# Two of three Newton-Schulz transposes moved from TensorE to the DMA queue, the third product one step later, three buffers, and a reordered first tile

## The chip, the cores and the metric

The kernel runs on one core of one Trainium2 chip. The metric is the device time in microseconds (us); lower is better.

## The reference, cut to what matters

The whole block is an adaptive layer norm, a test-time-training attention (LaCT SwiGLU) and a mixture of experts, for 8 sequences of 256 tokens and 256 features. Three weight gradients per head and sequence, 48 matrices of 128x128, are orthogonalised by five Newton-Schulz steps:

```
for a, b, c in NS_COEFFS:              # 5 steps
    A = X @ jnp.swapaxes(X, 1, 2)      # first product, needs X transposed
    Bm = b * A + c * (A @ A)           # second product
    X = a * X + Bm @ X                 # third product
```

Before it stand `h1 = layernorm(x) * (1 + scale) + shift` and `qkv = silu(h1 @ w_qkv.T)`, behind it the updated weights `w + dw`, the outputs, and the experts.

## The kernel before

It is one program in which each engine's instruction list is written out by hand, in order, with semaphores between them. An engine works strictly through its list, so a wait holds back everything behind it.

**First stage.** The input is normalised on VectorE (`xn`), transposed on TensorE (`xn_turned`, L872), scaled on ScalarE (`h1_out`, L597) and rounded there to a high part `h1hi` (L602); GpSimd makes the low part `h1lo` (L412). The product with `w_qkv` (L949) is three products for each tile of 128 tokens: high times high, low times high, high times low weights. Tile 0 begins after the transposes of sequences 0 and 1 and after `spin(4)` (L864), four matmuls whose result nobody reads. ScalarE makes the bfloat16 identities `identb` and `aI` (L653, L655) after `h1_out(1)`.

**Newton-Schulz.** The 48 matrices are 12 groups of 4 (`NGRP = 12`, `MPG = 4`), so 5 steps make `NR = 60` units n; group g = n % 12. The loop over r is a pipeline. In step r TensorE issues: the first product of unit r from `XT` (L1057, 4 matmuls), the second of unit r-1 from `Ar` (L1068, 4), the third of unit r-2 (L1081 and L1082, 8), and the transpose of the new X of unit r-3 (L1097, 4), which the first product of unit n+12 needs. ScalarE evicts the first product to `Ar` (L751) and the third to `X` (L759); VectorE makes `Br` (L1455) and evicts the transpose from PSUM to `XT` (L1464). `Ar` and `Br` have two buffers each. From unit 48 on nothing is transposed for a next step; there GpSimd adds X to the gradient (L547), and TensorE transposes the sum (L1040).

**SyncE's list.** It issues the DMAs in this order: the inputs; `weights(0)` and `weights(1)` (raw expert weights, 384 KB each); after GpSimd's `ga_ok` a small store and two broadcasts of 1,024 KB each into `wog` (L366); then `weights(2)`, `weights(3)`, `weights(4)`; then the DMAs of the expert stage. `raw` has two buffers, so `weights(j)` waits for GpSimd's `w_prep` number j-1, which GpSimd reaches in `split_weights(j-2)` (L523, L525), after the load j-2 has landed:

```
def weights(j):
    if j >= 2:
        sp.wait_ge(S["w_prep"], j - 1)
    sp.dma_start(raw[:, j % 2, :], moew_d[:, j, :]).then_inc(...)
```

Of the kernel before, what the change touches and what calls it, by code (L numbers as in the profile page):

```python
# [20 lines left out]
F32 = mybir.dt.float32  # L21
# [53 lines left out]
def build(nc, x_d, c_d, wmod_d, qkvw_d, w02_d, w1_d, wnat_d, wo_d, onw_d, gate_d, ident_d, moew_d, comb_d, out_d):  # L75
    ctx = ExitStack()
    with ctx:
# [53 lines left out]
        def carve(start, names):  # L131
# [27 lines left out]
        (XT, Ar, Br), end = carve(R_tmp, [  # L159
            ("XT", [P, NMAT, P], BF16), ("Ar", [P, 2, BLK], BF16), ("Br", [P, 2, BLK], BF16)])  # L160
        assert end <= R_wo
# [11 lines left out]
        assert end <= R_tmp + 20480  # L173
        wsq = [at("wsq0", [P, 6, P], F32, R_tmp + 16384), at("wsq1", [P, 6, P], F32, R_q + 12288)]
        (raw,), end = carve(R_tmp + 20480, [("raw", [P, 2, WCOLS], F32)])
# [56 lines left out]
        def bank(i):  # L232
# [5 lines left out]

            "const", "ident_ok", "silu_c", "mod_ps", "mod_sb", "mod_ok", "mod2_sb", "mod2_ok", "ga_ps", "ga_sb", "ga_ok", "wo_ok", "st_ga", "ld_ga", "wog_ok", "wn_ss", "wn_ok",

# [4 lines left out]

            "up_ps", "sig", "b_sg", "b_u", "b_ds", "b_dhb", "b_hid", "b_t", "b_dg", "b_kl", "b_vl", "dw_ps", "dw_sb",
            "xb_ok", "f_ss", "g_sq", "f_s7",

            "f_ps", "f_sum", "f_norm", "f_b", "f_inv", "x_init", "x_init_p", "t0_ps", "t0_a", "t0_v", "t_ps", "t_sb", "a_ps", "a_sb", "b_ps", "b_sb", "x_ps", "x_sb",
            "w_ok", "wt_ps", "wt_sb", "wsq_ok", "rss_ok", "rsq_ok", "ws_pow", "ws_chain", "ws_pool", "w_scale", "w_scale_p",  # L250
# [46 lines left out]
        def root_of(b):  # L297
            return b // 2 + 1 if b < 6 else b - 2

        def first_xt_ps(g):  # L300
# [36 lines left out]
        def _(sp):  # L337
# [30 lines left out]
            for j in range(2, CPG):  # L368
                weights(j)
            for n in range(NU):  # L370
                wg, blk, c, tok = unit(n)
                for half in range(2):
                    if n == half * (NBLK // 2) * CPG:
                        sp.wait_ge(S["ld_ga"], 16 * NH)
                        sp.wait_ge(S["combT_ok"], 2 * (half + 1))
                        cols = slice(half * T // 2, (half + 1) * T // 2)
                        sp.dma_start(comb_d[:, cols], combT[:, cols]).then_inc(S["st_comb"], 16)
                        sp.wait_ge(S["st_comb"], 16 * (half + 1))
                if n in turn:
# [18 lines left out]
        def _(po):  # L398
# [143 lines left out]
            for g in range(NGRP):  # L542
                if g == NGRP - 5:
                    row_roots(0)
                po.wait_ge(S["x_sb"], NGRP * (NS_STEPS - 1) + g + 1)
                wv = dw[:, g * MPG:(g + 1) * MPG, :]
                po.tensor_tensor(wv, wv, X[:, g * MPG:(g + 1) * MPG, :], ALU.add).then_inc(S["w_ok"], 1)  # L547
# [36 lines left out]
        def _(ac):  # L584
# [60 lines left out]
            ac.wait_ge(S["mod_ok"], 2)  # L645
            h1_out(0)
            for t in range(NT):
                blk, i = divmod(t, 4)
                if t % TPB == 0 and t // TPB + 1 < B:
                    h1_out(t // TPB + 1)  # L650
                if t == 0:
                    ac.wait_ge(S["ld_id"], 16)
                    ac.activation(identb[:, :], ident[:, :], ACT.Copy).then_inc(S["ident_ok"], 1)  # L653
                    for k in range(NS_STEPS):
                        ac.activation(aI[:, k, :], ident[:, :], ACT.Copy, scale=NS[k][0]).then_inc(S["ident_ok"], 1)  # L655
                if t < NT:
# [86 lines left out]
            for r in range(NGRP * NS_STEPS + 2):  # L743
# [3 lines left out]
                if n < NGRP * NS_STEPS:  # L747
                    ac.wait_ge(S["a_ps"], n + 1)
                    if n >= 2:
                        ac.wait_ge(S["b_sb"], n - 1)  # L750
                    ac.activation(Ar[:, n % 2, :], bank(n % 2), ACT.Copy, scale=NS[n // NGRP][1]).then_inc(S["a_sb"], 1)  # L751
                for g in TURN_AT.get(r - 1, ()):
                    if g % 2 == 0:
                        first_turned(g)
                n = r - 2
                if n >= 0:
                    g = n % NGRP
                    ac.wait_ge(S["x_ps"], n + 1)
                    ac.activation(X[:, g * MPG:(g + 1) * MPG, :], bank(4 + n % 2).rearrange("p (a d) -> p a d", d=P),  # L759
                                  ACT.Copy).then_inc(S["x_sb"], 1)  # L760
                if r == NGRP * NS_STEPS - 5:
# [87 lines left out]
        def _(pe_):  # L849
# [80 lines left out]
            for t in range(NT + 1):  # L930
                blk, i = divmod(t, 4)
                if t % TPB == 0 and t // TPB + 1 < B:
                    xn_turned(t // TPB + 1)
                if t == 0:
                    spin(4)
                if t < NT:
# [4 lines left out]
                    pe_.wait_ge(S["h1_hi"], b + 1)  # L941
                    for k, (h_, w_) in enumerate(((h1hi, qkvhi), (h1lo, qkvhi), (h1hi, qkvlo))):
                        if k == 1:
                            pe_.wait_ge(S["h1_lo"], b + 1)
                        for c in range(KC):
                            if t == 0 and k != 1:
                                pe_.wait_ge(S["qw_hi" if k == 0 else "qw_lo"], c + 1)
# [84 lines left out]
            def weights_turned(g):  # L1032

                pe_.wait_ge(S["w_ok"], g + 1)
                if g >= 2:
                    pe_.wait_ge(S["wt_sb"], g - 1)
                else:
                    pe_.wait_ge(S["t_sb"], NR - NGRP)
                for a in range(MPG):
# [3 lines left out]
            for r in range(NR + 2):  # L1043
                n = r
                if n < NR:
                    g = n % NGRP
                    if n >= NGRP:
                        pe_.wait_ge(S["t_sb"], n + 1 - NGRP)
                    else:
# [10 lines left out]
                if 0 <= n < NR:  # L1060
# [5 lines left out]
                    for a in range(MPG):  # L1066
                        Am = Ar[:, n % 2, a * P:(a + 1) * P]
                        last = mm(bank(2 + n % 2)[:, a * P:(a + 1) * P], Am, Am, start=True, stop=True)  # L1068
                    last.then_inc(S["b_ps"], 1)
                n = r - 2  # L1070
                if 0 <= n < NR:
                    g = n % NGRP
                    pe_.wait_ge(S["b_sb"], n + 1)
                    if n >= 2:
                        pe_.wait_ge(S["x_sb"], n - 1)
                    else:
                        pe_.wait_ge(S["t0_v" if n else "t0_a"], 3)
                    for a in range(MPG):
                        o = bank(4 + n % 2)[:, a * P:(a + 1) * P]
                        Xm = X[:, g * MPG + a, :]  # L1080
                        mm(o, aI[:, n // NGRP, :], Xm, start=True, stop=False)  # L1081
                        last = mm(o, Br[:, n % 2, a * P:(a + 1) * P], Xm, start=False, stop=True)  # L1082
                    last.then_inc(S["x_ps"], 1)
                n = r - 3
                if 0 <= n < NR - NGRP:
                    g, m = n % NGRP, NGRP + n
                    pe_.wait_ge(S["x_sb"], n + 1)
                    if n >= 2:
                        pe_.wait_ge(S["t_sb"], n - 1)
                    if n in (0, 6):  # L1090
# [56 lines left out]
            for g in range(NGRP - 4, NGRP - 2):  # L1147
                weights_turned(g)
            pe_.wait_ge(S["x_sb"], NR)
            outputs(0)  # L1150
# [96 lines left out]
        def _(ve):  # L1247
# [89 lines left out]
            def gate_products(b):  # L1337

                i = b % 2
                ve.tensor_tensor(hid[i][:, :, :], sg[:, :, :], hid_ps(i), ALU.mult).then_inc(S["b_hid"], 1)  # L1340
                ve.tensor_tensor(dhb[i][:, :, :], sg[:, :, :], dh_ps(i), ALU.mult).then_inc(S["b_dhb"], 1)

# [100 lines left out]
            for r in range(NR + 1):  # L1443
# [6 lines left out]
                if 0 <= n < NR:  # L1450
                    ve.wait_ge(S["b_ps"], n + 1)
                    if n >= 2:
                        ve.wait_ge(S["x_ps"], n - 1)
                    _, b_, c_ = NS[n // NGRP]
                    ve.scalar_tensor_tensor(out=Br[:, n % 2, :], in0=bank(2 + n % 2), scalar=c_ / (b_ * b_), in1=Ar[:, n % 2, :],  # L1455
                                            op0=ALU.mult, op1=ALU.add).then_inc(S["b_sb"], 1)
                if r == 1:
                    ve.wait_ge(S["g_sq"], 1)
                    ve.tensor_reduce(fss[:, 6 * (B - 1):], gsq[:, :, :], AX.X, ALU.add).then_inc(S["f_s7"], 1)
                n = r - 3  # L1460
                if 0 <= n < NR - NGRP:
                    g, m = n % NGRP, NGRP + n
                    ve.wait_ge(S["t_ps"], n + 1)
                    ve.tensor_copy(XT[:, g * MPG:(g + 1) * MPG, :], xt_ps(m)).then_inc(S["t_sb"], 1)  # L1464
# [228 lines left out]
```

## Time and profile before

| | |
|---|---|
| median of 3 runs | 683.43 us (682.58 to 685.45) |
| the profiled execution's own time | 680.91 us |
| its span, first to last instruction | 679.1 us |
| TensorE busy | 652.2 us (96%) |
| VectorE, ScalarE, GpSimd busy | 475.2, 337.0, 227.4 us |
| mean granted clock of TensorE | 0.994 |

The span is what the trace covers; 1.8 us of the execution's own time lie around it. The busy share is an average over very unlike stages: Newton-Schulz takes roughly 120 to 199 us of the span, the experts everything from 295 us on.

### The profile page before, as it was taken

Reading aid. Unit: us, or ns where it says so; the run is one execution under the profiler, and the core shown is the slowest. Engines: PE = TensorE matmul, PEld = TensorE weight load, DVE = VectorE, ACT = ScalarE, POOL = GpSimd, SP = SyncE. Lnnn points to the kernel's source line nnn. Section 1 sums busy time; section 2 is a strip of 40 time slices with the busy share of each in tenths; the row PEclk is TensorE's granted clock in tenths of the full one; section 3 lists DMA queues with packets and bytes.
Section 4 is the critical chain, followed back from the end, with each engine's and each line's share of the span. In section 5 each row is a group of like instructions: output and inputs, shape, how many; then the busy total and the mean of one; then the engine's idle time right before and its main releaser. Section 6 shows DMA issues by size and latency. Waiting matters only on the chain.

```text
span 679.1 us, 11544 instructions
## 1 busy us (share of the span) xinstructions
PE 652.2 (96%) x4146; PEld 561.1 (83%) x4146; DVE 475.2 (70%) x925; ACT 337.0 (50%) x721; POOL 227.4 (33%) x221
## 2 busy tenths in 40 slices
PE   8999998799978999999999999999999999999997
PEld 7889898699966888888888888888888888888885
DVE  6988878899987787774457665566656565555545
ACT  3778699799976864532332222332222332222331
POOL 4578868858267641241003310123002330000000
PEclk7999999999999999999999999999999999999999
DMA  8000000150000000340023322243122342212132
GB/s 327 5 1 1 1 2 3 45 173 27 2 2 0 2 1 1 102 116 29 19 80 92 114 84 70 75 125 109 63 64 84 109 115 71 62 64 69 55 91 111
DMA packets 23095, 43.58 MB, mean 64 GB/s; under 512 B 3544, under 2 KB 5856, under 8 KB 22912
## 3 DMA queue, kind: packets, MB, share of 16 engines
q1 hardware_dynamic: 22624, 42.26, 19.8%
q8 instruction: 34, 0.56, 0.3%
q10 hardware_dynamic: 416, 0.59, 0.3%
q14 instruction: 21, 0.17, 0.1%
HBM read 40.60 MB, written 2.24 MB: 63 GB/s over the span
## 4 chain that ended last, share of the span: by engine, by line
PE 76%; DVE 10%; ACT 5%; POOL 5%; issue 2%; DMA 2%; DVEq 0%; SPq 0%; ACTq 0%; POOLq 0%
PE ps L1143 38%; PE ps L1220 19%; PE ps L949 3%; PE ps L1057 2%; PE ps L1068 2%; PE ps L1081 2%; PE ps L1082 2%; PE ps L990 2%; PE ps L1097 2%; PE ps L1186 1%; DVE x L1583 1%; ACT junk L712 1%; PE ps L1166 1%; POOL qk L433 1%; PE ps L918 1%
## 5 line engine op out<-in xcount | busy, mean ns | idle before, releaser
L842 ACT ACTIVATE sgm<-ps,zero 128x512 f32<-128x512 f32 x100 | 68.9, 690 | 273.0 <-PE ps L1143 273.0
L1143 PE MATMUL ps<-h2hi,whi 128*128 128x512 f32 x400 | 156.1, 390 | 0.0
L1143 PE MATMUL ps<-h2lo,whi 128*128 128x512 f32 x400 | 155.6, 389 | 0.0
L1143 PE MATMUL ps<-h2hi,wlo 128*128 128x512 f32 x400 | 155.6, 389 | 0.0
L1634 DVE TENSOR_TENSOR am<-sgm,ps 128x512 f32<-128x512 f32 x88 | 60.5, 688 | 135.6 <-ACT sgm L842 135.6
L523 POOL CAST whi<-raw 128x768 fp32r<-128x768 f32 x25 | 21.7, 866 | 242.0 <-DMA raw<-in_moew 242.0
L1143 PEld LDWEIGHTS ps<-h2lo,whi 128*128 128x128 f32 x400 | 75.1, 188 | 15.7
L1143 PEld LDWEIGHTS ps<-h2hi,whi 128*128 128x128 f32 x400 | 75.1, 188 | 15.5
L1143 PEld LDWEIGHTS ps<-h2hi,wlo 128*128 128x128 f32 x400 | 75.1, 188 | 15.3
L1643 DVE TENSOR_TENSOR pm<-am,cw 128x512 f32<-128x512 f32 x88 | 74.9, 851 | 5.2 <-DMA cw<-combine 2.8
L1220 PE MATMUL ps<-ahi,whi 128*128 128x512 f32 x200 | 77.9, 390 | 0.1
L1220 PE MATMUL ps<-alo,whi 128*128 128x512 f32 x200 | 77.8, 389 | 0.0
L1220 PE MATMUL ps<-ahi,wlo 128*128 128x512 f32 x200 | 77.8, 389 | 0.0
L1598 DVE TENSOR_TENSOR alo<-pm,ahi 128x512 fp32r<-128x512 f32 x100 | 74.7, 747 | 0.2
L832 ACT ACTIVATE ahi<-pm 128x512 fp32r<-128x512 f32 x100 | 62.3, 623 | 1.8 <-DVE pm L1643 1.0
L525 POOL TENSOR_TENSOR wlo<-raw,whi 128x768 fp32r<-128x768 f32 x25 | 47.6, 1905 | 2.0
L1220 PEld LDWEIGHTS ps<-ahi,whi 128*128 128x128 f32 x200 | 37.5, 188 | 8.3 <-DVE alo L1598 0.5
L1455 DVE SCALAR_TENSOR_TENSOR Br<-ps,Ar 128x512 bf16<-128x512 f32 x60 | 41.4, 690 | 4.2 <-PE ps L1068 3.1
L1220 PEld LDWEIGHTS ps<-alo,whi 128*128 128x128 f32 x200 | 37.5, 188 | 7.8
L1220 PEld LDWEIGHTS ps<-ahi,wlo 128*128 128x128 f32 x200 | 37.5, 188 | 7.7
L751 ACT ACTIVATE Ar<-ps 128x512 bf16<-128x512 f32 x60 | 35.5, 593 | 4.1 <-DVE Br L1455 2.5
L759 ACT ACTIVATE X<-ps 128x512 bf16<-128x512 f32 x60 | 35.9, 598 | 2.8 <-PE ps L1082 0.8
(212 smaller groups left out, 1187.0 us busy)
## 6 DMA issues: line engine op xcount, KB each, us to landing
raw<-in_moew SPq DMA_DIRECT2D x25, 384.0 KB, 3.9
cw<-combine SPq DMA_DIRECT2D x32, 256.0 KB, 3.2
cw<-combine SPq DMA_DIRECT2D x16, 224.0 KB, 2.9
cw<-combine SPq DMA_DIRECT2D x16, 192.0 KB, 2.8
cw<-combine SPq DMA_DIRECT2D x16, 160.0 KB, 2.7
wog<-combine SPq DMA_DIRECT2D x2, 1024.0 KB, 7.0
cw<-combine SPq DMA_DIRECT2D x16, 128.0 KB, 3.0
out<-x1T SPq DMA_DIRECT2D x8, 256.0 KB, 3.7
```

The costliest lines, as they stand in the source:

```text
L523: po.tensor_copy(whi[wg % 2][:, c, :], raw[:, j % 2, :]).then_inc(S["w_hi"], 1)
L525: po.tensor_tensor(wlo[wg % 2][:, c, :], raw[:, j % 2, :], whi[wg % 2][:, c, :].bitcast(F32), ALU.subtract).then_inc(S["w_prep"], 1)
L751: ac.activation(Ar[:, n % 2, :], bank(n % 2), ACT.Copy, scale=NS[n // NGRP][1]).then_inc(S["a_sb"], 1)
L759: ac.activation(X[:, g * MPG:(g + 1) * MPG, :], bank(4 + n % 2).rearrange("p (a d) -> p a d", d=P), ACT.Copy).then_inc(S["x_sb"], 1)
L832: ac.activation(ahi[:, n % 4, :], pm[:, n % 3, :], ACT.Copy).then_inc(S["e_hi"], 1)
L842: ac.activation(sgm[:, n % 2, :], gate_bank(n), ACT.Silu, bias=zero[:, :]).then_inc(S["e_sg"], 1)
L1143: last = mm(o, w_, a_[:, kc, tok], start=(kc == 0 and k == 0), stop=(kc == KC - 1 and k == 2))
L1220: last = mm(bank(6 + f), w_, a_, start=(c == 0 and k == 0), stop=(c == CPG - 1 and k == 2))
L1455: ve.scalar_tensor_tensor(out=Br[:, n % 2, :], in0=bank(2 + n % 2), scalar=c_ / (b_ * b_), in1=Ar[:, n % 2, :], op0=ALU.mult, op1=ALU.add) ...
L1598: ve.tensor_tensor(alo[:, n % 3, :], pm[:, n % 3, :], ahi[:, n % 4, :].bitcast(F32), ALU.subtract).then_inc(S["e_lo"], 1)
L1634: ve.tensor_tensor(am[:, n % 2, :], sgm[:, n % 2, :], lin_bank(n), ALU.mult).then_inc(S["e_a"], 1)
L1643: ve.tensor_tensor(pm[:, n % 3, :], am[:, n % 2, :], cw[:, k % 3, :], ALU.mult).then_inc(S["e_p"], 1)
```

## The change

- **Transposes.** `BY_DMA` is the list of units n from 13 to 47 that 3 does not divide: 24 units. Their X is transposed into `XT` by `dma_start_transpose`, issued by SyncE, one for each unit (128x512 bfloat16, 128 KB). The other 24 (`ON_PE`) stay on TensorE and VectorE. SyncE's new loop stands behind `weights(4)`. Four semaphores (`xt_ld0` to `xt_ld3`) let four such DMAs be in flight.
- **Third product.** For units 14 to 47 it is issued in step n+3 and no longer in n+2, with the transpose, where there is one, in step n+4.
- **Buffers.** `Ar` and `Br` have three (`DEEP = 3`); `wsq0` moves to other SBUF bytes, since `Ar` and `Br` now lie where it was.
- **Evictions.** X of units 16, 20, ... 44 (8 units, `ON_VECTOR`) is evicted by VectorE and no longer by ScalarE.
- **First tile.** `spin(4)` is removed; sequence 1 is transposed after tile 0's high product and no longer ahead of it; ScalarE makes the identities ahead of `h1_out(1)`. For all tiles the product with the low input comes last. Two semaphore increments that nobody waits for are removed.

```diff
-            ("XT", [P, NMAT, P], BF16), ("Ar", [P, 2, BLK], BF16), ("Br", [P, 2, BLK], BF16)])
+            ("XT", [P, NMAT, P], BF16), ("Ar", [P, 3, BLK], BF16), ("Br", [P, 3, BLK], BF16)])
...
+        DEEP = 3
+        def lag(n):
+            return 3 if 14 <= n < NGRP * (NS_STEPS - 1) else 2
+        def evicted_at(r):
+            return [n for n in (r - 3, r - 2) if 0 <= n < NGRP * NS_STEPS and n + lag(n) == r]
+        def turned_at(r):
+            return [n for n in (r - 4, r - 3) if 0 <= n < NGRP * (NS_STEPS - 1) and n + lag(n) + 1 == r]
+        BY_DMA = [n for n in range(13, NGRP * (NS_STEPS - 1)) if n % 3]
+        ON_PE = [n for n in range(NGRP * (NS_STEPS - 1)) if n not in BY_DMA]
+        ON_VECTOR = range(16, NGRP * (NS_STEPS - 1), 4)
...
             for j in range(2, CPG):
                 weights(j)
+            for k, n in enumerate(BY_DMA):
+                g = n % NGRP
+                if k >= 4:
+                    sp.wait_ge(*turned_by(BY_DMA[k - 4]))
+                sp.wait_ge(*made(n))
+                sp.dma_start_transpose(XT[:, g * MPG:(g + 1) * MPG, :], X[:, g * MPG:(g + 1) * MPG, :]).then_inc(turned_by(n)[0], 16)
...
             h1_out(0)
+            ac.wait_ge(S["ld_id"], 16)
+            ac.activation(identb[:, :], ident[:, :], ACT.Copy).then_inc(S["ident_ok"], 1)
+            for k in range(NS_STEPS):
+                ac.activation(aI[:, k, :], ident[:, :], ACT.Copy, scale=NS[k][0]).then_inc(S["ident_ok"], 1)
...
-                    if n >= 2:
-                        ac.wait_ge(S["b_sb"], n - 1)
-                    ac.activation(Ar[:, n % 2, :], bank(n % 2), ACT.Copy, scale=NS[n // NGRP][1]).then_inc(S["a_sb"], 1)
+                    if n >= DEEP:
+                        ac.wait_ge(S["b_sb"], n + 1 - DEEP)
+                    ac.activation(Ar[:, n % DEEP, :], bank(n % 2), ACT.Copy, scale=NS[n // NGRP][1]).then_inc(S["a_sb"], 1)
...
-                if t == 0:
-                    spin(4)
...
-                    for k, (h_, w_) in enumerate(((h1hi, qkvhi), (h1lo, qkvhi), (h1hi, qkvlo))):
-                        if k == 1:
+                    for k, (h_, w_) in enumerate(((h1hi, qkvhi), (h1hi, qkvlo), (h1lo, qkvhi))):
+                        if k == 2:
                             pe_.wait_ge(S["h1_lo"], b + 1)
+                        if t == 0 and k == 1:
+                            xn_turned(1)
...
                     if n >= NGRP:
-                        pe_.wait_ge(S["t_sb"], n + 1 - NGRP)
+                        pe_.wait_ge(*turned_by(n - NGRP))
...
+                for n in [n for n in evicted_at(r) if n in ON_VECTOR]:
+                    g = n % NGRP
+                    ve.wait_ge(S["x_ps"], n + 1)
+                    ve.tensor_copy(X[:, g * MPG:(g + 1) * MPG, :], bank(4 + n % 2).rearrange("p (a d) -> p a d", d=P)).then_inc(S["x_sv"], 1)
```

`made(n)` is the semaphore and count that say that X of unit n is written; `turned_by(n)` is the same for its transpose.

## Rows read from the trace of the kernel before

**Rows 1.** Windows: length, busy of PE, PEld, DVE, ACT, POOL, clock, DMA, GB/s.

```profile
152.40:182.10 29.70, 29.70 (x536) 29.70 (x534) 29.14 (x54) 28.86 (x54) 15.22 (x13) 1.00 0.06 16
...
256.00:679.00 423.00, 417.53 (x1870) 345.18 (x1868) 258.98 (x463) 132.73 (x217) 58.75 (x43) 1.00 0.26 79
```

**Rows 2.** Groups by line from 152.4 to 181.3 us, Newton-Schulz steps 25 to 50.

```profile
L1455 DVE SCALAR_TENSOR_TENSOR Br<-ps,Ar 128x512 bf16<-128x512 f32 x27 | 18.7, 692 | 0.6
L759 ACT ACTIVATE X<-ps 128x512 bf16<-128x512 f32 x26 | 15.5, 597 | 0.8
L751 ACT ACTIVATE Ar<-ps 128x512 bf16<-128x512 f32 x26 | 15.4, 591 | 0.0
...
L1464 DVE COPY XT<-ps 128x512 bf16<-128x512 bf16 x26 | 11.1, 426 | 0.0
L1097 PE MATMUL ps<-identb,X 128*128 128x128 bf16 x105 | 10.3, 219 | 0.0
```

**Rows 3.** Timeline of TensorE: first products of units 16, 25, 51 and 58.

```profile
142.14 0.39 PE L1057 MATMUL ps<-XT 128*128 128x128 bf16 x4
...
152.45 0.39 PE L1057 MATMUL ps<-XT 128*128 128x128 bf16 x4
...
181.48 0.39 PE L1057 MATMUL ps<-XT 128*128 128x128 bf16 x4
...
190.69 0.39 PE L1057 MATMUL ps<-XT 128*128 128x128 bf16 x4
```

**Rows 4.** Timeline of SyncE's queue: the broadcasts, weights(2) to weights(4), and weights(4) alone.

```profile
139.37 1.02 SPq L366 DMA_DIRECT2D wog<-combine  x2
140.71 12.20 SPq L357 DMA_DIRECT2D raw<-in_moew  x3
...
152.59 0.33 SPq L357 DMA_DIRECT2D raw<-in_moew  x1
```

**Rows 5.** Timeline of GpSimd: split_weights(2), and the next start on load 4.

```profile
149.83 0.82 POOL L523 CAST whi<-raw 128x768 fp32r<-128x768 f32 x1 [6.48 <-DMA raw<-in_moew]
150.74 1.82 POOL L525 TENSOR_TENSOR wlo<-raw,whi 128x768 fp32r<-128x768 f32 x1
...
155.74 0.82 POOL L523 CAST whi<-raw 128x768 fp32r<-128x768 f32 x1 [0.52 <-DMA raw<-in_moew]
```

**Rows 6.** DMA issues: size of each, median us from issue to landing.

```profile
raw<-in_moew SPq DMA_DIRECT2D x25, 384.0 KB, 3.9
...
cw<-combine SPq DMA_DIRECT2D x16, 128.0 KB, 3.0
...
combine<-combT SPq DMA_DIRECT2D x2, 64.0 KB, 1.9
```

**Rows 7.** Timeline of the first tile, ScalarE and TensorE.

```profile
11.29 0.63 ACT L602 ACTIVATE h1hi<-h1T 128x512 fp32r<-128x512 f32 x1
...
10.96 1.12 PE L872 MATMUL ps<-ident,xn 128*128 128x128 f32 x4 [0.82 <-DVE xn L1271]
11.87 1.92 PE L864 MATMUL ps<-ones 128*128 128x128 f32 x8
13.44 1.64 PE L949 MATMUL ps<-qkvhi,h1hi 128*128 128x512 f32 x4
...
16.63 0.87 PE L949 MATMUL ps<-qkvhi,h1hi 128*128 128x512 f32 x4
```

**Rows 8.** Windows of the clock, columns as in rows 1.

```profile
9.00:12.00 3.00, 2.12 (x9) 1.76 (x10) 2.83 (x4) 1.65 (x3) 1.76 (x3) 0.50 1.01 420
...
15.00:16.00 1.00, 1.00 (x6) 0.86 (x5) 1.00 (x7) 0.00 (x0) 1.00 (x2) 0.71 1.01 403
...
200.00:202.00 2.00, 0.42 (x2) 0.43 (x3) 2.00 (x5) 1.95 (x3) 1.33 (x1) 1.00 0.00 0
```

**Rows 9.** Timeline of tile 8's second and third product on TensorE.

```profile
37.65 0.99 PE L949 MATMUL ps<-qkvhi,h1lo 128*128 128x512 f32 x4 [1.46 <-POOL h1lo L412]
38.47 0.87 PE L949 MATMUL ps<-qkvlo,h1hi 128*128 128x512 f32 x4
```

More of the change, by code:

```diff
@@ L173, in build @@
         assert end <= R_tmp + 20480
-        wsq = [at("wsq0", [P, 6, P], F32, R_tmp + 16384), at("wsq1", [P, 6, P], F32, R_q + 12288)]
+        wsq = [at("wsq0", [P, 6, P], F32, R_x1T + T * 4 - 6 * P * 4), at("wsq1", [P, 6, P], F32, R_q + 12288)]
         (raw,), end = carve(R_tmp + 20480, [("raw", [P, 2, WCOLS], F32)])
@@ L237, in build @@
             "ld_x0", "ld_xa", "ld_xb", "ld_xc", "ld_mod", "ld_mod2", "ld_id", "ld_qkv0", "ld_qkv1", "ld_c", "ld_wn", "ld_w", "ld_raw0", "ld_raw1", "st_out",
-            "const", "ident_ok", "silu_c", "mod_ps", "mod_sb", "mod_ok", "mod2_sb", "mod2_ok", "ga_ps", "ga_sb", "ga_ok", "wo_ok", "st_ga", "ld_ga", "wog_ok", "wn_ss", "wn_ok",
+            "const", "ident_ok", "silu_c", "mod_ps", "mod_ok", "mod2_sb", "mod2_ok", "ga_ps", "ga_sb", "ga_ok", "wo_ok", "st_ga", "ld_ga", "wog_ok", "wn_ss", "wn_ok",
             "stat1", "agg1", "var1", "rs_ok", "xn_ok", "tr_ps", "h1_ok", "h1_hi", "h1_lo", "qw_hi", "qw_lo",
@@ L244, in build @@
             "lr_z", "lr_e", "lr_c", "lr_ok",
-            "up_ps", "sig", "b_sg", "b_u", "b_ds", "b_dhb", "b_hid", "b_t", "b_dg", "b_kl", "b_vl", "dw_ps", "dw_sb",
+            "up_ps", "sig", "b_sg", "b_u", "b_ds", "b_t", "b_dg", "b_kl", "b_vl", "dw_ps", "dw_sb",
             "xb_ok", "f_ss", "g_sq", "f_s7",
-            "f_ps", "f_sum", "f_norm", "f_b", "f_inv", "x_init", "x_init_p", "t0_ps", "t0_a", "t0_v", "t_ps", "t_sb", "a_ps", "a_sb", "b_ps", "b_sb", "x_ps", "x_sb",
+            "f_ps", "f_sum", "f_norm", "f_b", "f_inv", "x_init", "x_init_p", "t0_ps", "t0_a", "t0_v", "t_ps", "t_sb", "xt_ld0", "xt_ld1", "xt_ld2", "xt_ld3", "a_ps", "a_sb", "b_ps", "b_sb", "x_ps", "x_sb", "x_sv",
             "w_ok", "wt_ps", "wt_sb", "wsq_ok", "rss_ok", "rsq_ok", "ws_pow", "ws_chain", "ws_pool", "w_scale", "w_scale_p",
@@ L298, in root_of, with turned_by, made @@
             return b // 2 + 1 if b < 6 else b - 2
+        DEEP = 3
[8 more added lines that the diff above has]
+        ON_VECTOR = range(16, NGRP * (NS_STEPS - 1), 4)
+        def turned_by(n):
+            if n not in BY_DMA:
+                return S["t_sb"], ON_PE.index(n) + 1
+            k = BY_DMA.index(n)
+            return S[f"xt_ld{k % 4}"], 16 * (k // 4 + 1)
+        def made(n):
+            vector = len([k for k in ON_VECTOR if k <= n])
+            return (S["x_sv"], vector) if n in ON_VECTOR else (S["x_sb"], n + 1 - vector)
         def first_xt_ps(g):
@@ L544, in _ @@
                     row_roots(0)
-                po.wait_ge(S["x_sb"], NGRP * (NS_STEPS - 1) + g + 1)
+                po.wait_ge(*made(NGRP * (NS_STEPS - 1) + g))
                 wv = dw[:, g * MPG:(g + 1) * MPG, :]
@@ L650, in _ @@
                     h1_out(t // TPB + 1)
-                if t == 0:
[L652 to L655, printed above, removed]
                 if t < NT:
@@ L754, in _ @@
                         first_turned(g)
-                n = r - 2
-                if n >= 0:
+                for n in evicted_at(r):
                     g = n % NGRP
-                    ac.wait_ge(S["x_ps"], n + 1)
-                    ac.activation(X[:, g * MPG:(g + 1) * MPG, :], bank(4 + n % 2).rearrange("p (a d) -> p a d", d=P),
-                                  ACT.Copy).then_inc(S["x_sb"], 1)
+                    if n not in ON_VECTOR:
+                        ac.wait_ge(S["x_ps"], n + 1)
+                        ac.activation(X[:, g * MPG:(g + 1) * MPG, :], bank(4 + n % 2).rearrange("p (a d) -> p a d", d=P),
+                                      ACT.Copy).then_inc(S["x_sb"], 1)
                 if r == NGRP * NS_STEPS - 5:
@@ L931, in _ @@
                 blk, i = divmod(t, 4)
-                if t % TPB == 0 and t // TPB + 1 < B:
+                if t and t % TPB == 0 and t // TPB + 1 < B:
                     xn_turned(t // TPB + 1)
-                if t == 0:
-                    spin(4)
                 if t < NT:
@@ L941, in _ @@
                     pe_.wait_ge(S["h1_hi"], b + 1)
-                    for k, (h_, w_) in enumerate(((h1hi, qkvhi), (h1lo, qkvhi), (h1hi, qkvlo))):
-                        if k == 1:
+                    for k, (h_, w_) in enumerate(((h1hi, qkvhi), (h1hi, qkvlo), (h1lo, qkvhi))):
+                        if k == 2:
                             pe_.wait_ge(S["h1_lo"], b + 1)
+                        if t == 0 and k == 1:
+                            xn_turned(1)
                         for c in range(KC):
-                            if t == 0 and k != 1:
+                            if t == 0 and k < 2:
                                 pe_.wait_ge(S["qw_hi" if k == 0 else "qw_lo"], c + 1)
@@ L1037, in weights_turned @@
                 else:
-                    pe_.wait_ge(S["t_sb"], NR - NGRP)
+                    pe_.wait_ge(S["t_sb"], len(ON_PE))
                 for a in range(MPG):
@@ L1066, in _ @@
                     for a in range(MPG):
-                        Am = Ar[:, n % 2, a * P:(a + 1) * P]
+                        Am = Ar[:, n % DEEP, a * P:(a + 1) * P]
                         last = mm(bank(2 + n % 2)[:, a * P:(a + 1) * P], Am, Am, start=True, stop=True)
                     last.then_inc(S["b_ps"], 1)
-                n = r - 2
-                if 0 <= n < NR:
+                for n in evicted_at(r):
                     g = n % NGRP
@@ L1074, in _ @@
                     if n >= 2:
-                        pe_.wait_ge(S["x_sb"], n - 1)
+                        pe_.wait_ge(*made(n - 2))
                     else:
@@ L1081, in _ @@
                         mm(o, aI[:, n // NGRP, :], Xm, start=True, stop=False)
-                        last = mm(o, Br[:, n % 2, a * P:(a + 1) * P], Xm, start=False, stop=True)
+                        last = mm(o, Br[:, n % DEEP, a * P:(a + 1) * P], Xm, start=False, stop=True)
                     last.then_inc(S["x_ps"], 1)
[L1084 to L1089, printed above, removed]
+                for n in [n for n in turned_at(r) if n in ON_PE]:
+                    g, m = n % NGRP, ON_PE.index(n)
+                    pe_.wait_ge(*made(n))
+                    if m >= 2:
+                        pe_.wait_ge(S["t_sb"], m - 1)
                     if n in (0, 6):
@@ L1148, in _ @@
                 weights_turned(g)
-            pe_.wait_ge(S["x_sb"], NR)
+            pe_.wait_ge(*made(NR - 1))
             outputs(0)
@@ L1339, in gate_products @@
                 i = b % 2
-                ve.tensor_tensor(hid[i][:, :, :], sg[:, :, :], hid_ps(i), ALU.mult).then_inc(S["b_hid"], 1)
-                ve.tensor_tensor(dhb[i][:, :, :], sg[:, :, :], dh_ps(i), ALU.mult).then_inc(S["b_dhb"], 1)
+                ve.tensor_tensor(hid[i][:, :, :], sg[:, :, :], hid_ps(i), ALU.mult)
+                ve.tensor_tensor(dhb[i][:, :, :], sg[:, :, :], dh_ps(i), ALU.mult)
             ve.wait_ge(S["v_sb"], 2 * NT)
@@ L1451, in _ @@
                     ve.wait_ge(S["b_ps"], n + 1)
-                    if n >= 2:
-                        ve.wait_ge(S["x_ps"], n - 1)
+                    if n >= DEEP:
+                        ve.wait_ge(S["x_ps"], n + 1 - DEEP)
                     _, b_, c_ = NS[n // NGRP]
-                    ve.scalar_tensor_tensor(out=Br[:, n % 2, :], in0=bank(2 + n % 2), scalar=c_ / (b_ * b_), in1=Ar[:, n % 2, :],
+                    ve.scalar_tensor_tensor(out=Br[:, n % DEEP, :], in0=bank(2 + n % 2), scalar=c_ / (b_ * b_), in1=Ar[:, n % DEEP, :],
                                             op0=ALU.mult, op1=ALU.add).then_inc(S["b_sb"], 1)
@@ L1459, in _ @@
                     ve.tensor_reduce(fss[:, 6 * (B - 1):], gsq[:, :, :], AX.X, ALU.add).then_inc(S["f_s7"], 1)
[L1460 to L1463, printed above, removed]
+                for n in [n for n in evicted_at(r) if n in ON_VECTOR]:
+                    g = n % NGRP
+                    ve.wait_ge(S["x_ps"], n + 1)
+                    ve.tensor_copy(X[:, g * MPG:(g + 1) * MPG, :], bank(4 + n % 2).rearrange("p (a d) -> p a d", d=P)).then_inc(S["x_sv"], 1)
+                for n in [n for n in turned_at(r) if n in ON_PE]:
+                    g, m = n % NGRP, ON_PE.index(n)
+                    ve.wait_ge(S["t_ps"], m + 1)
                     ve.tensor_copy(XT[:, g * MPG:(g + 1) * MPG, :], xt_ps(m)).then_inc(S["t_sb"], 1)
```

## The prediction

> **What bounds the kernel now.** I read the windows by stage first. The experts, from 256 us on, keep TensorE busy 417.5 of 423 us, and the change does not touch them [rows 1]. In Newton-Schulz steps 25 to 50, TensorE is busy all of 29.7 us at the full clock, but VectorE (29.1) and ScalarE (28.9) are too: taking work from one engine alone would gain little [rows 1]. The groups by line say what a step holds: one Br (692 ns) and one XT copy (426 ns) on VectorE, one Ar (591) and one X (597) on ScalarE [rows 2]. The timeline gives the step: first product of unit 25 at 152.45, of unit 51 at 181.48, so 26 steps in 29.03 us, 1.117 us each; with 20 matmuls of 128 columns in a step that is 55.8 ns a matmul [rows 3].
>
> Then I looked at SyncE's queue, since the transposes are to stand in it. The last of weights(2) to weights(4) is issued only at 152.59 and takes 0.33 us, up to 152.92 [rows 4]. It waits for GpSimd's split of load 2, which ends at 150.74 + 1.82 = 152.56; and that split waited 6.48 us for load 2, which had been queued behind the two 1,024 KB broadcasts [rows 4, 5].
>
> **The change, part by part.** All times are those of the profile before, 680.91 us, which is 2.5 us below the median of 683.43.
>
> *First tile.* The rounding of h1hi ends at 11.29 + 0.63 = 11.92, but the first product starts at 13.44, behind four spins [rows 7]. Without them it can start at about 12.0. At half clock (0.50 up to about 15.6) tile 0 then takes 1.3 us for the high product (twice 774 columns at 1.2 GHz), 0.9 for the transposes of sequence 1 (10.96 to 11.87 before), 1.3 for the next and, if the clock rises at 15.6 as before, 0.7 for the last: 16.2 where tile 1 starts at 16.63 now [rows 7, 8]. Gain 0.4 us. The identities on ScalarE lie in the time in which it waits for those transposes; without that cover they would cost their own 1.4 us. If the missing spins let the clock stay low, 1.3 us are lost in place of the 0.4.
>
> *Low input last.* At tile 8 TensorE waits 1.46 us for h1lo and then runs two products from 37.65 on, the first 0.82 us long up to 38.47 [rows 9]. With the low product last, the other one fits into the wait: gain 0.7 us, as TensorE is followed by work that hangs on it. First part together: -1.1 us.
>
> *Newton-Schulz, work.* From the first product of unit 25 to that of unit 51, before: 520 matmuls. After: first and second products 26 x 8 = 208, third products of units 22 to 48 are 27 x 8 = 216 (one more, since it lags by a step), transposes of 21, 24, ... 45 are 9 x 4 = 36: 460 x 55.8 ns = 25.7 us. ScalarE keeps 26 Ar and 21 X: 27.9 us by durations, which overlap in the trace (30.9 us of them in the 28.9 us window), so about 26.1 [rows 2]. VectorE: 26 x 0.692, 9 x 0.426 and 6 copies of X. That copy is not in the trace; it reads 512 float32 columns of PSUM as Br does (0.69, the value I take; bound below the XT copy, 0.43): 26.0 us. All three fall together, so the move is balanced. I take 26.5 us, 2.5 less than 29.03; bounds 25.7 and 28. The third buffers and the later third product make room for these uneven steps; they add no instruction and I price them at nothing. If the slack were missing, steps with two VectorE evictions would stretch by up to 0.4 us, twice in these 26 steps.
>
> *Newton-Schulz, the late start.* Unit 25's first product needs the transpose of unit 13, the first by DMA. TensorE comes to it early: from unit 16 at 142.14 it has 144 matmuls (two units of transposes in place of nine, eight third products in place of nine), 8.0 us, and with 0.5 for the other engines it stands there at about 150.7. But SyncE is in weights(4) until 152.92. The landing is not in the trace. Bound below: the 64 KB store, 1.9 us, gives 154.8. Bound above: a 128 KB load, 3.0 us, counted only from load 4's landing at 155.7 (GpSimd starts on it at 155.74), gives 158.7 [rows 5, 6]. The same 384 KB lie ahead in the same queue, so I take a little behind their landing: 156.3. Against 152.45 now that is 3.8 us late; TensorE idles 5.6 us, and Ar, Br and every X behind it wait too.
>
> So unit 51 begins at 156.3 + 26.5 = 182.8 in place of 181.48: +1.3 us. After it nothing changes: a unit from 48 on has no transpose in either kernel.
>
> *The clock.* The trace has no such idle gap of TensorE at this point. After a gap of 1.6 us (200 to 202, busy 0.42) it stays at 2.4 GHz. In the first stage it is at 1.2 GHz from before 9 us, with TensorE little busy; work without a break begins at 10.96, and the clock is up only at about 15.6 [rows 7, 8]. 4.6 us at half rate cost 2.3 us. An idle time of 5.6 us is far beyond 1.6, so I take the fall and add 2.3; bounds 0 and 3.3 (all of 9.0 to 15.6 at half rate). The Trainium skill, page "TensorE: Matmul & The Clock Gate", Part 1, says that the throttled state is the default and activity releases it; by it the fall is the rule and the sum keeps its 2.3, and by the 200 us row alone the sum would be 2.3 lower.
>
> *Later transposes.* After the first, a DMA turn is needed every 1.5 steps, 1.5 us; four may be in flight, so landing in up to 6 us is hidden. The queue must take one in 1.5 us. Plain issues take 0.33 to 0.5 us on SyncE [rows 4]. I price these at nothing; see the second rival for the other case.
>
> Sum: -1.1 + 1.3 + 2.3 = +2.5 us: 683.4 on the profile's scale, 685.9 as a median. The first case: chance 0.35, own range 0 to +6.
>
> **Rivals.**
>
> *The clock holds.* Same lateness, no fall: -1.1 + 1.3 = +0.2 us, 683.6 (range -2 to +4). For it: the short gaps keep the clock. Chance 0.22.
>
> *The queue is the bound.* If a transpose has to finish before the next gets through, 23 of them follow the first. At the smallest landing, 1.9 us, that is 43.7 us: unit 46 is turned at 156.3 + 43.7 = 200.0, where unit 58 starts at 190.69 now [rows 3, 6]. +9.3 - 1.1 = +8.2 us, 691.6. At 3.0 us each: +33.5, 717. It decides from about 1.5 us a transpose. Against it: four are in flight, and the queue is otherwise empty. Chance 0.24. The Trainium skill is of two minds: "VectorE: DVE Perf Modes", The three transpose paths, gives 1309 ns for one 128x128 by DMA, from which I estimate 5.2 us for a group of four; 23 of these one after another would be 120 us, some 85 us slower; "Advanced Engine Details and Errata", X-Bar Transpose, calls such DMAs as fast as regular ones. No row here shows either.
>
> *Not late at all, faster.* If load 2 lands early enough for SyncE to be free by 148.8, unit 25 starts at 150.7 and unit 51 at 177.2: -4.3 - 1.1 = -5.4 us, 678.0. It decides where the first transpose lands before 152.7. For it: the wait hangs on how the broadcasts and load 2 share the queue, which another execution may order otherwise. Against: 152.92 is SyncE's time even for the issue. Chance 0.13.
>
> *The clock stays low at the start.* 1.7 us on top of the first case: +4.2, 687.6. Chance 0.06.
>
> **How the numbers follow.** A difference of 0.5% (3.4 us) is about what a measurement can tell from no change. Slower by more: the queue rival 0.24, the start's clock 0.04, a third of the first case 0.12: 0.40. Faster by more: 0.13. Same: 0.47. The range 679 to 694 leaves out about half of the faster rival and the longer half of the queue rival.
>
> **What would show it.** After: one idle time of TensorE of 4 to 7 us ahead of L1057 at unit 25, ended by the DMA XT<-X, starting near 150; SyncE's first transpose directly behind weights(4); a granted clock of 0.5 behind it for some us; steps of about 1.0 us; only 96 matmuls of transpose in this loop, 24 XT copies, 8 X copies on VectorE; no wait for h1lo at tile 8 or one 0.7 shorter; tile 1 starting near 16.2. Wrong it is if repeated DMA waits stand ahead of L1057 (queue), or none (not late), or if steps stay at 1.1 us.

## The result, and the profile after

| | before | changed |
|---|---|---|
| median of 20 runs each, side by side | 684.54 us (681.04 to 688.00) | 687.37 us (685.74 to 689.93) |
| ratio, with its 95% interval | | 1.005 [1.0039, 1.0061] |
| the profiled execution | 680.91 us | 687.8 us |
| its span | 679.1 us | 686.0 us |

The changed kernel is slower by 0.5% (0.39 to 0.61%): 2.8 us between the medians, where +2.5 was forecast. That is the difference of about 0.5% which the prediction takes as hard to tell from no change. The two profiled executions lie 6.9 us apart, since the one of before is 3.6 us below its own median of 20; I come back to that in the account.

TensorE's wait for a DMA in Newton-Schulz after the change, with sum, count and longest. Before, no wait for a DMA stood there at all:

```profile
PE ps L1087 <- DMA XT<-X: 4.7, 1, 4.7
```

There is one wait and it is not repeated. L1087 is the first product (L1057 before). The timeline of TensorE shows which one, and what follows; the rows to set beside it are [rows 3]:

```profile
151.48 0.22 PE L1111 MATMUL ps<-X,Br 128*128 128x128 bf16 x1
...
156.45 0.61 PE L1087 MATMUL ps<-XT 128*128 128x128 bf16 x4 [4.75 <-DMA XT<-X]
...
158.56 0.63 PE L1087 MATMUL ps<-XT 128*128 128x128 bf16 x4
...
161.69 0.39 PE L1087 MATMUL ps<-XT 128*128 128x128 bf16 x4
...
185.91 0.39 PE L1087 MATMUL ps<-XT 128*128 128x128 bf16 x4
...
196.73 0.39 PE L1087 MATMUL ps<-XT 128*128 128x128 bf16 x4
```

Unit 25 starts at 156.45 after an idle time of 4.75 us. Its four matmuls take 0.61 us and those of unit 26 at 158.56 take 0.63; only at 161.69, unit 28, do four take 0.39 again. Unit 51 is at 185.91, unit 59 at 196.73. The windows around it (the number before the DMA share is the granted clock) say why:

```profile
152.00:154.00 2.00, 0.00 (x0) 0.00 (x0) 0.29 (x1) 0.34 (x1) 1.92 (x3) 1.00 0.29 26
154.00:156.00 2.00, 0.00 (x0) 0.00 (x0) 0.00 (x0) 0.00 (x0) 1.38 (x2) 0.64 0.96 279
156.00:158.00 2.00, 1.55 (x15) 1.55 (x16) 0.48 (x1) 0.60 (x1) 1.92 (x2) 0.50 0.44 89
158.00:160.00 2.00, 2.00 (x22) 2.00 (x20) 0.98 (x3) 1.20 (x2) 2.00 (x3) 0.50 0.61 123
160.00:162.00 2.00, 2.00 (x27) 2.00 (x25) 0.98 (x3) 1.09 (x2) 2.00 (x2) 0.66 0.36 74
```

The mean of 0.64 in the second window puts the fall to 1.2 GHz at about 154.6, some 3 us into the idle time; by the 0.66 of the last window the clock is back at 2.4 GHz at about 161.4. SyncE's queue gives the reason for the idle time, beside [rows 4]:

```profile
140.62 12.22 SPq L382 DMA_DIRECT2D raw<-in_moew  x3
152.89 35.33 SPq L400 DMA_TRANSPOSE XT<-X  x24
```

The three loads keep SyncE until 152.84, and the first transpose goes out right behind them. The transposes themselves, by tile (issue ns min/median/max, then issue to landing in us):

```profile
L400 SPq DMA_TRANSPOSE XT<-X x24: 1188/1219/2295, 152.9 to 187.0; - x24
...
DMA to landing us min/median/max: 2.4/2.5/4.3
```

An issue occupies SyncE for 1.22 us at the median, and half of the transposes land within 2.5 us of their issue (in e1, below, the median is 3.4). The first lands 3.5 us after its issue, at 156.4.

### The profile page after: what moved, and what is told of

Its sections match the earlier page's. It is cut to its first block, busy times and chain, and to the rows that moved or that the text cites. A ratio compares the mean times of both kernels' runs of the same rounds, so it can differ in the third digit from the quotient of the medians.

```text
span 686.0 us, 11330 instructions
## 1 busy us (share of the span) xinstructions
PE 653.8 (95%) x4042; PEld 560.0 (82%) x4042; DVE 468.2 (68%) x909; ACT 333.5 (49%) x713; POOL 229.1 (33%) x221
## 4 chain that ended last, share of the span: by engine, by line
PE 75%; DVE 8%; POOL 6%; ACT 4%; DMA 4%; issue 3%; SPq 0%; DVEq 0%; ACTq 0%; POOLq 0%
PE ps L1171 38%; PE ps L1248 18%; PE ps L979 4%; PE ps L1214 2%; PE ps L928 2%; DVE x L1614 1%; DMA raw<-in_moew 1%; PE ps L1020 1%; PE ps L1098 1%; PE ps L948 1%; PE ps L1194 1%; PE ps L1110 1%; PE ps L1111 1%; PE ps L1087 1%; DMA x<-in_x 1%
## 5 line engine op out<-in xcount | busy, mean ns | idle before, releaser
L1629 DVE TENSOR_TENSOR alo<-pm,ahi 128x512 fp32r<-128x512 f32 x100 | 77.3, 773 | 0.2
L1674 DVE TENSOR_TENSOR pm<-am,cw 128x512 f32<-128x512 f32 x88 | 72.0, 818 | 5.8 <-DMA cw<-combine 3.4
L1110 PE MATMUL ps<-X,aI 128*128 128x128 bf16 x240 | 34.1, 223 | 1.4 <-DVE Br L1483 1.4
```

The costliest lines, as they stand in the source:

```text
L1629: ve.tensor_tensor(alo[:, n % 3, :], pm[:, n % 3, :], ahi[:, n % 4, :].bitcast(F32), ALU.subtract).then_inc(S["e_lo"], 1)
L1674: ve.tensor_tensor(pm[:, n % 3, :], am[:, n % 2, :], cw[:, k % 3, :], ALU.mult).then_inc(S["e_p"], 1)
```

## The experiments

Each ran beside the kernel before; ratios are to it, with the 95% interval. Edits are to the changed kernel unless said otherwise. In e1, f1, f3, g1 and g2 line numbers are two higher from the edit on.

**e1: the fifth expert load stands behind seven transposes,** those of units 13 to 22.

```diff
-            for j in range(2, CPG):
+            for j in range(2, CPG - 1):
                 weights(j)
             for k, n in enumerate(BY_DMA):
                 g = n % NGRP
+                if n == 23:
+                    weights(CPG - 1)
```

> The changed kernel, but SyncE issues weights(4) only behind the transposes of units 13 to 22, so that the first transpose no longer stands behind a load that is issued at 152.6. If the lateness of the first transpose and the clock that falls in the wait are what the change costs: no wait for a DMA above 1.5 us ahead of unit 25, unit 25 begins at 150.7 to 152 and not at 156.4, unit 51 near 178.5 and not 185.9, the clock stays at 2.4 GHz, and the kernel is 6 to 8 us faster than the changed one and about 3.5 us (0.5%) faster than before. If the DMA transposes themselves are too slow or disturb the other engines, the waits move to later units and the time stays within 1.5 us of the changed kernel.

680.12 us, 0.9935 [0.9913, 0.9957]: 1% faster than the changed kernel and 0.65% faster than before. SyncE's queue and the first products of units 25 and 51 in e1:

```profile
142.60 12.02 SPq L402 DMA_TRANSPOSE XT<-X  x7
154.67 0.57 SPq L382 DMA_DIRECT2D raw<-in_moew  x1
155.35 25.83 SPq L402 DMA_TRANSPOSE XT<-X  x17
```

```profile
150.49 0.39 PE L1089 MATMUL ps<-XT 128*128 128x128 bf16 x4
...
177.78 0.39 PE L1089 MATMUL ps<-XT 128*128 128x128 bf16 x4
```

The same 24 transposes, one load moved past seven of them: no wait for a DMA, unit 25 at 150.49 in place of 156.45, 26 steps in 27.29 us. Of these 6.0 us, 4.9 are the change's: from unit 16 to unit 25 it takes 9.63 us in place of 14.54, and this execution reached unit 16 1.05 us earlier. So the order of SyncE's list is the cause of the lateness, and transposing by DMA is not the bound.

**e2: no transpose by DMA until unit 19.**

```diff
-        BY_DMA = [n for n in range(13, NGRP * (NS_STEPS - 1)) if n % 3]
+        BY_DMA = [n for n in range(19, NGRP * (NS_STEPS - 1)) if n % 3]
```

> The changed kernel, but the first unit turned by DMA is 19 and no longer 13 (20 DMAs in place of 24); SyncE's list keeps its order. Unit 19's transpose is needed by unit 31, which TensorE would reach near 157.3, and SyncE issues at 152.9. If lateness is the cost: landing near 156.4 is in time, wait below 1 us, 6 us faster than the changed kernel (0.9 us of the gain goes back to TensorE for four transposes), about 3 us faster than before. If the rate of the queue or contention is the cost: four DMAs fewer of 24 give back a sixth of it at most, below 1 us.

680.93 us, 0.9942 [0.992, 0.9965]. The loads stay where they are and the first unit that needs a transpose by DMA is 31. Its first product in the timeline:

```profile
160.36 0.40 PE L1087 MATMUL ps<-XT 128*128 128x128 bf16 x4 [0.26 <-DMA XT<-X]
```

The wait shrinks from 4.75 to 0.26 us. Moving the need has nearly the same effect as moving what stood ahead in the queue.

**e5: matmuls in the wait.** TensorE gets 85 matmuls on the identity ahead of unit 25, whose results are unused; the rest of the computation is whole.

```diff
+                    if n == 25:
+                        pe_.wait_ge(S["a_sb"], n - 1)
+                        for _ in range(85):
+                            mm(bank(n % 2)[:, 0:P], identb[:, :], identb[:, :], start=True, stop=True)
```

> The changed kernel with 85 extra matmuls of 128 columns (4.7 us, result unused, overwritten) ahead of the wait of unit 25 for its transpose. The wait for the DMA is as long, TensorE is busy in it. If the clock that falls in the wait costs 2.3 us beside the wait: the clock stays at 2.4 GHz, unit 25 begins at 156.4 as in the changed kernel, unit 51 2.3 us earlier than there, and the time is 2.3 us below it. If the slow clock only takes time that the other engines or the later transposes would have taken anyway: within 0.7 us of the changed kernel.

685.27 us, 1.0006 [0.9988, 1.0024], against 1.005 [1.0039, 1.0061] for the changed kernel. Timeline of TensorE, then two windows:

```profile
152.23 4.91 PE L1080 MATMUL ps<-identb 128*128 128x128 bf16 x85
157.32 0.40 PE L1091 MATMUL ps<-XT 128*128 128x128 bf16 x4 [0.18 <-DMA XT<-X]
```

```profile
154.00:156.00 2.00, 2.00 (x40) 2.00 (x37) 0.00 (x0) 0.00 (x0) 1.88 (x2) 1.00 0.78 206
158.00:160.00 2.00, 2.00 (x39) 1.99 (x37) 1.76 (x4) 1.90 (x4) 2.00 (x2) 1.00 0.59 103
```

Unit 25 is no earlier (SyncE is through with the loads only at 153.66 here, 0.8 us later than in the changed kernel's trace), but the clock stays at 1.00 and its four matmuls take 0.40 us, not 0.61. From unit 25 to unit 59 it takes 38.35 us, where the changed kernel takes 40.28: the fall of the clock costs 1.9 us, by itself. The medians give 2.1, where the expectation had 2.3.

**f3: every transpose by DMA** (with e1's order of the loads): `BY_DMA` holds all 35 units from 13 to 47.

> e1_load4_behind with every unit from 13 to 47 turned by DMA, 35 in place of 24. SyncE takes 1.22 us to issue one transpose in the changed kernel's trace, and one would be needed in each step of 1.0 us. If that issue time is what limits the queue: SyncE issues without a break, falls behind by 0.2 us a unit, TensorE waits for DMAs at late units, some 2 us in all or steps of 1.2 us at the end, and it is 0 to 3 us slower than e1. If the queue has room (landing 2.5 us, four in flight), there are no such waits and it is 1 to 2 us faster than e1, with transposes gone from TensorE.

690.80 us, 1.0083 [1.0055, 1.0112]. TensorE's waits, then fifteen transposes in SyncE's timeline:

```profile
PE ps L1089 <- DMA XT<-X: 9.1, 14, 2.0
```

```profile
163.88 21.16 SPq L402 DMA_TRANSPOSE XT<-X  x15
```

That is 1.41 us for each transpose: thirteen of the fifteen issues take 1.22 us each, with the next one 1.31 us after their start, and two take about 2.0. In this stretch SyncE waits for nothing, neither for an X nor for a landing. With one needed in every step of about 1 us this is the bound, and 14 first products wait. The expectation named the cause and had the size wrong: 0.2 us behind in each step and 0 to 3 us in all, where the 26 steps take 37.20 us (1.43 each) and the medians are 10.7 us above e1. With two in three, as in the change, one is needed every 1.5 steps, and e1 shows no such wait.

**g1: every X on ScalarE** (e1, with `ON_VECTOR = range(0)`).

> e1_load4_behind with all evictions of X on ScalarE (no X copies on VectorE). My sum has ScalarE at 26 Ar and 21 X in these 26 steps; with 27 X it is 31.5 us by durations, 29.4 as they overlapped in the trace, 1.13 us a step: the gain of the moved transposes is lost. Steps of 1.1 us, 2 to 3 us slower than e1. Rival: ScalarE's durations overlap more than I counted, TensorE sets the pace, same time as e1.

680.48 us, 0.9949 [0.9931, 0.9967]; 27.57 us for the 26 steps against 27.29. The 2 to 3 us did not come: the eight copies on VectorE buy 0.3 us in the traces and nothing that the medians resolve.

**g2: third product not later** (e1, with the lag always 2).

```diff
-            return 3 if 14 <= n < NGRP * (NS_STEPS - 1) else 2
+            return 2
```

> e1_load4_behind with the third product of every unit in step n+2, as before the change; transposes by DMA, X copies on VectorE and three buffers stay. I priced the later third product at nothing and said that without the slack the steps with two evictions on VectorE would stretch by up to 0.4 us. If so: TensorE waits for VectorE's Br ahead of the third product in some of these steps, 0.5 to 2 us slower than e1. If the slack is not needed: same time as e1 within 0.5 us.

680.90 us, 0.9952 [0.9934, 0.9970]. TensorE's waits for Br in g2, then in e1:

```profile
PE ps L1112 <- DVE Br L1485: 2.3, 6, 0.9
```

```profile
PE ps L1112 <- DVE Br L1485: 1.4, 3, 0.9
```

The 26 steps take 27.73 us, and they hold one third product (0.45 us) less than e1's 27.29: 0.9 us for the later third product. From unit 16 to unit 59, where both kernels have the same work, the difference is 0.6 us (48.31 against 47.72), and f1, whose loop is e1's, takes 47.25 there. The three waits more are of 0.3 us each and lie in the steps where the lag differs. So the slack is worth some 0.6 to 0.9 us in the traces; the medians, 0.8 us apart, have intervals that overlap.

**f2: third product and buffers alone** (`BY_DMA = []`, `ON_VECTOR = range(0)`).

> The changed kernel with every transpose back on TensorE and every eviction of X back on ScalarE: left are the third product one step later, the three buffers and the first part. My sum prices lag and buffers at nothing: steps stay at 1.117 us, no wait of TensorE above 0.5 us in the Newton-Schulz loop, time within 1 us of before (-0.7 by the low input, +0.4 by the first tile). If the later third product or the buffers had an effect of their own on the pace, the 26 steps from unit 25 to 51 would differ from 29.03 us by more than 0.5.

683.47 us, 0.9977 [0.9957, 0.9997], the first part of the change included. The 26 steps take 29.48 us; less the extra third product, 0.45, that is the 29.03 of before. Without the transposes by DMA the later third product and the buffers give nothing to the loop. The run is 1.0 us below the kernel before by the medians, 1.6 us by the ratio (0.2 to 2.9), and what is left to cause it is the first part.

**f4: low input last, alone** (the kernel before, with the order of the three products changed).

> The kernel before with one edit, the product with the low input last in every tile. Theory: at tile 8 the wait for h1lo falls from 1.46 to 0.75 us and the gain of 0.7 us goes through to the end: 0.7 us (0.1%) faster. Rival: another wait behind it takes it up, no difference above 0.2 us.

683.25 us, 0.9975 [0.9953, 0.9996]. Timeline at tile 8, beside [rows 9]:

```profile
37.17 0.99 PE L949 MATMUL ps<-qkvhi,h1lo 128*128 128x512 f32 x4 [0.76 <-POOL h1lo L412]
```

The wait for h1lo falls from 1.46 to 0.76 us. No later wait takes it up in the first stage: from the first product of tile 1 to that of tile 15 it takes 39.83 us, before 40.45. The run is 1.2 us faster by the medians, 1.7 us by the ratio (0.3 to 3.2), which includes the 0.7 expected.

**e4: the first tile as before**, with the spins, sequence 1 transposed ahead of tile 0, and the identities behind `h1_out(1)`; the low input stays last.

> The changed kernel with the first tile of before: spin(4) back, sequence 1 transposed ahead of tile 0, identities behind h1_out(1); the low input stays last. If the missing spins keep the clock low up to 18 us: the clock rises near 15.6 again, tile 1 starts 0.5 to 1 us earlier, and the kernel is 0.5 to 1 us faster than the changed one. If the changed first tile is a gain as I priced it: 0.4 us slower than the changed one.

686.20 us, 1.0024 [1.0004, 1.0045]. **f1**, the same on e1:

> e1_load4_behind with the first tile of before (spins, sequence 1 turned ahead of tile 0); the low input stays last. In e1's trace the clock rose at about 16.1, not at 18 as in the changed kernel's, so the new first tile loses less there. If the spins still pay: 0.3 to 1 us faster than e1 (680.1), 679.5. If they only cost their place: 0.4 us slower than e1.

680.53 us, 0.9942 [0.9921, 0.9964], against e1's 0.9935. On one base the old order looks 0.3% better, on the other 0.1% worse, with intervals that overlap both times. The traces agree: tile 1 starts at 16.13 to 17.18 in the four profiles with the old order and at 16.39 to 17.21 in the nine with the new one. The first tile's new order is worth nothing that these runs resolve.

**g3: the changed kernel once more**, under g1 and g2's conditions.

> The changed kernel itself, beside the next two on one chip: 0.5% above before, one wait of 4 to 6 us ahead of unit 25, as in its first trace.

686.96 us, 1.0038 [1.0022, 1.0054], with the same single wait in the waits of TensorE:

```profile
PE ps L1087 <- DMA XT<-X: 5.3, 1, 5.3
```

## Why the prediction came out right

**The late start.** Forecast: TensorE at unit 25 from 150.7, first product at 156.3, 5.6 us idle. Measured: there from 151.7, first product at 156.45, 4.75 us idle. TensorE came 1.0 us later than forecast: from unit 16 on it stood 0.9 us in all for ScalarE's `Ar` (see the steps, below) and 0.5 us at a place where the profile names no cause. The mechanism is shown from two sides: e1 moves the load, e2 moves the need, and either takes nearly all of the wait away. The landing, 3.5 us after the issue, lies within the bounds of 1.9 and 5.8 us and near the value taken from load 4. The faster rival (not late at all) fell: in the four profiles that keep the loads ahead and start at unit 13 SyncE was free at 151.9 to 153.7, in none by 148.8.

**The clock.** Forecast: it falls, 4.6 us of work at half rate, 2.3 us. Measured: it falls, and from 156.45 to 161.4 are 4.9 us, 2.5 us by the sum's way of counting; e5 gives 1.9 back, and e1, which takes 38.09 us from unit 25 to unit 59, is 2.2 us shorter. The rival with the clock held fell. The row at 200 us with its 1.6 us gap was no guide to one of 4.75. The Trainium skill, "TensorE: Matmul & The Clock Gate", Part 1, counts the throttled state as the one the engine returns to when it does nothing; the trace agrees, 0.50 after this gap.

**The steps.** Forecast 26.5 us for 26, bounds 25.7 and 28. Measured 27.29 in e1, where no wait for a DMA disturbs them: 1.7 us gained on 29.03, not 2.5. This is the term that was mis-sized most. It was to come out of three engines that are equally full. The row of e1, beside [rows 1]:

```profile
150.40:177.70 27.30, 27.05 (x464) 25.73 (x462) 24.64 (x43) 24.77 (x48) 16.20 (x13) 1.00 0.61 107
```

In the sum VectorE and ScalarE now have 2.6 us to spare. The groups by line say what they wait for:

```profile
L1485 DVE SCALAR_TENSOR_TENSOR Br<-ps,Ar 128x512 bf16<-128x512 f32 x27 | 18.1, 687 | 2.7 <-PE ps L1100 2.5
L783 ACT ACTIVATE Ar<-ps 128x512 bf16<-128x512 f32 x27 | 16.2, 600 | 1.8 <-PE ps L1089 1.6
```

Yet TensorE, with 460 matmuls or 25.7 us of work at 55.8 ns, took 1.6 us more. Its busy 27.05 of 27.30 us hides that, since a matmul's record (0.22 us) is longer than the 55.8 ns after which the next one starts. The waits for Br (1.4 us over the whole loop in e1) are not it: they lie outside these steps, and before has the same 1.4. It shows in the start of the second product, here in the step of unit 31, TensorE, its weight load, then ScalarE:

```profile
156.61 0.39 PE L1089 MATMUL ps<-XT 128*128 128x128 bf16 x4
157.06 0.40 PE L1100 MATMUL ps<-Ar 128*128 128x128 bf16 x4
...
157.05 0.23 PEld L1100 LDWEIGHTS ps<-Ar 128*128 128x128 bf16 x4 [0.23 <-ACT Ar L783]
...
155.92 0.60 ACT L791 ACTIVATE X<-ps 128x512 bf16<-128x512 f32 x1
156.41 0.59 ACT L783 ACTIVATE Ar<-ps 128x512 bf16<-128x512 f32 x1
```

Where nothing holds it, the second product follows the start of the first by 0.22 us, as in all 26 steps before. Here it takes 0.45, and starts 0.06 us after the end of ScalarE's `Ar`, which had stood behind an X in ScalarE's list. In 8 of the 26 steps the second product is late in this way, by 0.08 to 0.23 us, 1.35 us in all. A step without a transpose is 0.89 us of TensorE's work, while an `Ar` and an X together take ScalarE 0.95 to 1.2 in e1. So the term that failed is the balance: the sums over 26 steps fall together, the single steps do not. The slack that was to cover these uneven steps, priced at nothing, covers them in part. Whether another order in ScalarE's list would give the 1.35 us back was not tried.

The copy of X on VectorE was forecast at 0.69 us; the source line of after:

```profile
L1491 DVE CAST X<-ps x8: 681/681/682, 146.1 to 182.9; 128x512 bf16<-128x512 f32 x8
```

In size right, but g1 shows that it was hardly needed: with six evictions more in these steps ScalarE holds TensorE up for only 0.3 us more. The later third product was priced at nothing and is worth 0.6 to 0.9 us in the trace of g2, less than the intervals tell; the other term of that sentence, the buffers, was not tried alone.

**The queue.** One transpose was not to take more than 1.5 us; this was the rival at 0.24. It fell, by a narrow margin: 1.22 us of SyncE per issue, where 0.33 to 0.5 was forecast from plain loads, and 1.41 us per transpose when they follow each other (f3). At 1.5 steps of 1.05 us, 1.57 us, they just keep up. That step of the working was wrong in size, and it was partly luck that the result did not suffer. The rival's own sum counts one transpose too many: 22 and not 23 follow the first up to that of unit 46. The Trainium skill, "Advanced Engine Details and Errata", X-Bar Transpose, has such DMAs as fast as regular ones: landing agrees (2.5 us at the median after the change and 3.4 in e1, where 128 KB loads of `cw` take 3.0 and 2.9), the issue does not (1.22 against 0.33 us). The estimate of 5.2 us for a group of four, from the 1309 ns that the Trainium skill gives in "VectorE: DVE Perf Modes", The three transpose paths, did not hold either: a group lands in 2.5 us and the next can follow 1.31 us later.

**The first part.** Forecast -1.1 us. The wait at tile 8 is 0.7 us shorter in f4, and 0.76 us is what is left of it in the changed kernel, as forecast. The whole part is in f2, whose loop is as long as before: 1.0 us faster by the medians, 1.6 by the ratio. The 0.4 us of the first tile did not show in the profile after: tile 1's first product starts at 17.21, not near 16.2, and by the windows the clock is low until 18:

```profile
16.00:18.00 2.00, 2.00 (x8) 1.71 (x8) 1.97 (x8) 1.11 (x2) 1.37 (x1) 0.50 0.66 270
18.00:20.00 2.00, 2.00 (x14) 1.78 (x13) 1.55 (x3) 0.66 (x4) 1.08 (x2) 1.00 0.01 4
```

That looks like the rival of the clock that stays low at the start. It is not shown to be the change's doing: over the profiles the clock rises at 14.6 to 16.7 with the old order and at 15.6 to 18.1 with the new one, the two overlap, and e4 and f1 don't resolve a cost. Tile 0 does start 1.1 to 1.6 us earlier (at 11.8 to 12.3, before at 13.44). In e2, where the clock rises at 15.6 as it did before, tile 1 starts at 16.39, 0.2 us earlier than before, where 0.4 was forecast.

**The sum.** In the trace unit 51 is 4.4 us later than before (+1.3 and +2.3 forecast, 3.6): the steps were 0.8 too cheap. Up to unit 59 the difference is 4.7 us, in g3 3.5. The work behind it, the same in both kernels, takes 489.3 us after and 487.1 before, and between 487.8 and 492.5 in the other profiles: 2.2 us of the 6.9 between the two profiled executions is this spread. Counted from unit 16 to unit 59, so that the start of each execution drops out, the loop costs 4.9 us in the changed kernel's trace and 4.6 in g3, where the forecast had 3.6. With f2's -1.0 to -1.6 for the first part that makes 3.0 to 3.9 us; 2.8 was measured between the medians and 3.4 (2.7 to 4.2) by the ratio. So the mechanism and the signs of all its large terms were right and the loop was about 1 us too cheap. That the medians come within 0.3 us of +2.5 is closer than the terms are known, and is in part luck.

**What stays open.** Why the clock rises at different times in the first stage, why two in fifteen issues of a transpose take 2.0 us and not 1.22, and what the buffers are worth alone.

## What to carry to other kernels

When a transfer joins a queue, read what stands ahead of it in that list and when that is through, before counting what the transfer saves: here the load ahead cost 4.9 us of start and 2 us of clock, and moving one load turned +0.5% into -0.65%. An idle time of some microseconds of TensorE is to be priced with the slow work behind it. Count the issue of a special DMA by its own kind: it was nearly four times that of a plain one, and the share of two in three was about all that the queue could take. And when work is balanced between engines, check it step by step: ScalarE's work fitted into the 26 steps with room to spare, and TensorE still waited for it in 8 of them.

## What the runs showed that was not expected

- SyncE is occupied 1.22 us by the issue of one 128x512 bfloat16 transpose, and the transposes follow each other at 1.41 us on average (f3).
- TensorE's clock falls within an idle time of 4.75 us, some 3 us after it began, and stays at 1.2 GHz for 4.9 us of work without a break afterwards; in e5 it stays at 2.4 GHz over the same time.
- Back-to-back evictions by ScalarE last 600 ns each by their records, but two of them take less than twice that of the engine's time: before, 30.9 us of durations lay in 28.9 us.
- An engine with 2.5 us to spare in 27.3 (ScalarE in e1) held up TensorE in 8 of 26 steps, and TensorE's busy time of 27.05 us did not show it; the wait stood at its weight load.
